# Attention and two gated networks on one core: the normed tokens turned on another path, the values a step later

## The reference, cut to what matters

```python
xn = layernorm(x)
# attention: 8 heads of 128, chunks of 128 tokens, linear attention with a running state
h  = rmsnorm(xn, attn_norm_w)
q, k, v = h @ Wq, h @ Wk, h @ Wv
for each chunk:                      # per head
    o = tril(q @ k.T) @ v + q @ S
    S = S + k.T @ v
o  = rmsnorm(o, attn_out_norm_w)     # per head
x2 = xn + o @ Wo
h2 = rmsnorm(x2, mlp_norm_w)
s  = x2 + (silu(h2 @ Wgate) * (h2 @ Wup)) @ Wdown
# second network: activations and weights rounded to FP4 in groups of 16
g  = silu(fp4_linear(silu(fp4_linear(xn, w_gate)) * fp4_linear(xn, w_up), w_down))
out = x + s * g
```

## Time and profile before

| | |
|---|---|
| median of 3 runs (lowest, highest) | 1065.48 us (1065.27, 1066.4) |
| the profiled execution | 1066.6 us |
| its span, first to last instruction | 1064.5 us |
| attention phase, 64 steps | 22 to 606 us |
| networks phase | 606 to 1064 us |
| TensorE / VectorE / ScalarE busy | 99% / 85% / 50% |
| granted TensorE clock, mean | 0.999 of full |
| DMA | 143 MB, 134 GB/s |

### The profile page before, as it was taken

One profiled execution on the slowest core, in us unless ns is written; L12 is line 12 of the kernel. 1 busy time (PEld: TensorE's weight loads), 2 busy tenths in 40 slices (PEclk: granted clock), 3 DMA queues, 4 the chain that ended last, 5 costly groups with the idle time before them and its releaser, 6 DMA issues.

```text
span 1064.5 us, 18767 instructions
## 1 busy us (share of the span) xinstructions
PE 1053.9 (99%) x6794; PEld 961.5 (90%) x6794; DVE 908.8 (85%) x1887; ACT 528.1 (50%) x1490; POOL 47.4 (4%) x68
## 2 busy tenths in 40 slices
PE   9999999999999999999999999999999999999998
PEld 5999999989999989989999889999999999999997
DVE  6788888888888888888888798888888888889887
ACT  6664655756656546557555634443333333243332
POOL 0000000000000000000000000101001010101010
PEclk9999999999999999999999999999999999999999
DMA  7445355455464553653544623253433233423213
GB/s 237 149 159 174 108 173 168 138 157 166 134 192 133 165 171 115 187 170 123 171 148 162 194 66 99 80 158 93 121 90 119 85 120 97 122 84 92 87 57 112
DMA packets 166173, 143.08 MB, mean 134 GB/s; under 512 B 28737, under 2 KB 162881, under 8 KB 166081
## 3 DMA queue, kind: packets, MB, share of 16 engines
q1 hardware_dynamic: 166080, 141.88, 42.7%
HBM read 77.27 MB, written 64.57 MB: 133 GB/s over the span
## 4 chain that ended last, share of the span: by engine, by line
PE 88%; DMA 6%; DVE 2%; ACT 2%; SPq 2%; issue 1%; DVEq 0%
PE ps L259 69%; PE ps L713 5%; PE ps L757 4%; PE ps L751 4%; PE ps L737 4%; DMA moved<-work 3%; DMA r_gate<-moved 2%; SPq L409 1%; PE ps L839 1%; PE ps L598 1%; SPq L481 1%; DMA work<-kept_w 1%; DMA work<-in_L_attn_hidden_states 0%; ACT work L922 0%; DVE work L1473 0%
## 5 line engine op out<-in xcount | busy, mean ns | idle before, releaser
L259 PE MATMUL ps<-r_k,r_gate_up 128*128 128x512 f32 x768 | 185.2, 391 | 0.5 <-DVE r_k L1537 0.5
L259 PEld LDWEIGHTS ps<-r_k,r_gate_up 128*128 128x128 f32 x768 | 141.5, 188 | 27.9 <-issue 0.7
L259 PE MATMUL ps<-r_o,onT 128*128 128x256 f32 x768 | 107.0, 289 | 0.4 <-DVE onT L1265 0.4
L259 PE MATMUL ps<-r_h,r_k 128*128 128x512 f32 (+1 forms) x393 | 105.2, 403 | 0.0
L259 PEld LDWEIGHTS ps<-r_q,r_v 128*128 128x128 f32 x768 | 99.7, 191 | 5.0 <-DVE r_v L1605 0.3
L259 PE MATMUL ps<-r_q,r_v 128*128 128x256 f32 x768 | 102.3, 283 | 0.0
L259 PE MATMUL ps<-r_h,r_q 128*128 128x512 f32 x384 | 98.2, 391 | 0.0
L946 ACT ACTIVATE work<-ps 128x128 f32<-128x128 f32 x256 | 67.0, 276 | 62.8 <-PE ps L757 62.7
L259 PE MATMUL ps<-r_v,r_h 128*128 128x512 f32 x384 | 97.4, 390 | 0.0
L259 PEld LDWEIGHTS ps<-r_o,onT 128*128 128x128 f32 x768 | 95.8, 190 | 0.8 <-DVE onT L1265 0.7
L922 ACT ACTIVATE work<-ps 128x512 f32<-128x512 f32 x64 | 38.3, 599 | 109.3 <-PE ps L259 109.1
(11 more groups left out here) (155 smaller groups left out, 1996.1 us busy)
## 6 DMA issues: line engine op xcount, KB each, us to landing
moved<-work SPq DMA_DIRECT2D x63, 512.0 KB, 2.9
r_gate<-moved SPq DMA_DIRECT2D x252, 128.0 KB, 2.5
kept_h<-work SPq DMA_DIRECT2D x31, 384.0 KB, 2.6
work<-kept_h SPq DMA_DIRECT2D x124, 96.0 KB, 2.3
work<-in_L_attn_hidden_states SPq DMA_DIRECT2D x16, 512.0 KB, 5.4
kept<-work SPq DMA_DIRECT2D x9, 514.0 KB, 4.4
kept_h<-work SPq DMA_DIRECT2D x9, 512.0 KB, 3.6
kept_xq<-work SPq DMA_DIRECT2D x8, 512.0 KB, 5.8
```

What stands on the lines that cost most here:

```text
L259: done = pe.matmul(out_ap, a, b, start=first and n == 0, stop=last and n == 2, skip_group_check=skip)
```

## The change

It does five things.

1. `turn_h` is gone from TensorE after the first block. VectorE turns `h_sb` in 32x32 blocks into `x_in` at step 3 (early), SP stores it to `kept_h` within that step's `exchange`, then loads it into `xq_new` in four parts behind that exchange; ScalarE and VectorE make the parts of `hT` from there at step 4.
2. The weight of the attention norm no longer scales `hT` but Wq, Wk and Wv, once at the start. `nw_attn` is loaded by a DMA on ScalarE's queue.
3. Values are made one step later than before (`values_of`), since `hT` is ready later. In steps 0 and 4 they stand between keys and queries.
4. VectorE's extras move: `x2_factor` from early to late step 3, the piece's scales from late step 7 to early step 0, its grid to late step 1, the rounding of x and the transposes of h2 about one step later. h2 is now normed in place in `x2`, after `x2` is stored, at step 5.
5. On SP's queue the store of h2 moves from step 5 to 6.

```diff
-                def exchange(value, o=None, turned_o=None, again=True):
+                def exchange(value, o=None, turned_o=None, again=True, next_h=None):
...
+                    if next_h is not None:
+                        sp.wait_ge(h_turned, KD + next_h)
+                        sp.dma_start(kept_h[next_h % HALVES].rearrange("a p x -> p a x"),
+                                     in_quads(x_in.rearrange("p c d -> p (c d)"))).then_inc(h_stored, 16)
                     if again:
                         sp.wait_ge(k_tok_ready, value - 1)
...
+                        if turns_h:
+                            if 1 <= n <= PIECES:
+                                sp.wait_ge(grid_read, n)
+                            if n:
+                                sp.wait_ge(xq_ready, n)
+                            sp.wait_ge(h_stored, 16 * (n + 1))
+                            load_turned(xq_new, kept_h[(n + 1) % HALVES], h_loaded)
...
+        def values_of(b, j):
+
+            h, s = j % H, j // H
+            if 0 < h <= CH:
+                return 1, h - 1, s
+            if h == 0:
+                return (0, CH - 1, s) if b or j else None
+            return (0, h - CH - 1, 1 - s) if b * HALVES + s < BLOCKS - 1 else None
...
-                    if h == CH and ahead:
-                        pe.wait_ge(hT_ready, (n0 + s) * KD + 2 * KD)
...
                         project(wk, B_K, h_next, s_next, k_done)
+                    v = values_of(b, j)
+                    if v is not None and h % CH == 0:
+                        pe.wait_ge(v_ready, t0 + j - 1 + CH)
+                        values(*v)
+                    if not (final and last):
                         project(wq, B_Q, h_next, s_next, q_done)
-                    pe.wait_ge(v_ready, min(CH, STEPS - j) + t0 + j if final else t0 + j + CH)
-                    if ahead or h < CH:
-                        values(*((1, h, s) if h < CH else (0, h - CH, 1 - s)))
+                    if v is not None and h % CH:
+                        if h == CH + 1:
+                            pe.wait_ge(hT_ready, (n0 + s) * KD + 2 * KD)
+                        pe.wait_ge(v_ready, t0 + j - 1 + CH)
+                        values(*v)
+                    if h % CH == 0:
+                        pe.wait_ge(v_ready, t0 + j + CH)
...
-                    if h == CH - 1 and ahead:
-                        pe.wait_ge(h_ready, n0 + s + 2)
-                        pe.wait_ge(k_perm_ready, t0 + j + 2)
-                        turn_h(0)
-                        pe.wait_ge(attn_ready, t0 + j + 1)
-                        turn_h(1)
...
+                def turned_hi(parity, n):
+                    act.wait_ge(h_loaded, 16 * QUADS * n)
+                    for k in range(KD):
+                        act.activation(as_tokens(hT[:, parity, HI, k, :]), landed(xq_new, k), ACT.Copy).then_inc(hT_hi, 1)
...
-                    if h == CH - 1 and ahead:
-                        turned_hi(0, 1 - s, (n0 + s) * KD + KD + 1)
-                        turned_hi(1, 1 - s, (n0 + s) * KD + KD + 2)
...
+                    if h == CH and ahead:
+                        turned_hi(1 - s, n0 + s + 1)
...
+                    if h == CH + 1 and ahead:
+                        normed_h2(n0 + s + 1, None)
...
                     if h == 0 and rounds_piece:
-                        dve.wait_ge(xq_ready, n)
-                        fp4_grid(piece, grid_w, mine)
+                        fp4_scales(piece, piece, scale, mine)
...
-                    if h == 3:
-                        x2_factor(n + 1, mine)
-                    if h == 3 and rounds_piece:
+                    if h == CH - 1 and rounds_piece:
                         fp4_add(piece, grid_w, mine, ALU.subtract)
+                        dve.sem_inc(grid_read, 1)
+                    if h == CH - 1 and ahead:
+                        dve.wait_ge(h_ready, n + 2)
+                        turn_blocks(x_in.rearrange("p c d -> p (c d)"), h_flat, h_turned)
...
                     if h == (0 if final else CH):
                         fp4_max(x_of_block, x_scale, mine)
-                    if h == CH + 1:
-                        if rounds_piece and n <= KD:
-                            weights4_lo(n - 1, h_flat[:, 0:N4])
-                            dve.wait_ge(w4_ready, n)
-                        elif rounds_piece:
+                    if h == (0 if final else CH + 1):
+                        fp4_factor(x_scale, mine)
+                    if h == CH + 2 and not final:
+                        if n > KD and rounds_piece:
                             dve.wait_ge(piece_stored, 16 * (n - KD))
-                        if not final:
-                            turn_h2(n)
-                    if h == CH + 2 and not final:
-                        fp4_add(xq_new, grid_x, mine)
+                        turn_h2(n, x2[:, :, 0:D])
                     if h == CH + 3 and not final:
-                        dve.wait_ge(h2_stored, 16 * n + 16)
-                        turn_xq(n)
+                        fp4_scaled(xq_new, x_scale).then_inc(x_rounded, 1)
...
-                    if h == CH - 1 and ahead:
-                        turned_lo(0, 1 - s, n * KD + KD + 1)
-                        turned_lo(1, 1 - s, n * KD + KD + 2)
+                    if h == CH - 1:
+                        x2_factor(n + 1, mine)
                     if h == CH - 1 and rounds_piece:
                         settled(fp4_scaled(piece, scale), mine)
+                    if h == CH and ahead:
+                        turned_lo(1 - s, n + 1)
```

## The result

The kernel after took 1068.86 us at the median (1065.76 to 1071.31 in 20 runs) beside 1066.09 for the kernel before on the same chip (1064.17 to 1068.97 in 20). The ratio is 1.0024, 95% interval 1.0015 to 1.0033: slower by 2.6 us where I had forecast 3.9 faster, and above the 1066.5 at which my range ended. A second timing gave 1.0011 (0.9999 to 1.0024), so the loss is 1 to 3 us. The profiled execution has a span of 1067.1 beside 1064.5.

The account below looks back on a forecast made before the run. TensorE, busy 99% of the span, was taken as the bound, VectorE second. Terms -6.1 + 2.1 - 1.6 + 1.7 - 0.3 + 0.3 = -3.9 gave a median of 1061.6 us; 8-in-10 range 1059 to 1066.5.

Parts of the forecast that it names:

- The transposes and their cover: Step 3: eight TensorE transposes gone in blocks 0 to 6, -6.1; state sums then late in blocks 1 to 6, +2.1.
- Step 5: Blocks 1 to 3: weight-split and h2 transposes leave the place ahead of the state sums, -1.6.
- The new transfers: Store and loads of turned tokens on SP's queue, steps 3 and 4: land before ScalarE comes at 6.4, cost 0.
- Rival 2: Added transfers slow only exchanges, delaying turn_k of step 5: +2 to +5 in all, no change that can be told; chance 0.26.
- Step 4's order: Step 4 of the odd blocks: VectorE's chain begins 0.1 later, adding 0.2.
- Step 6: 2.6 to 3.5 of rounding behind step 5's sums; step 6's sums still reached under the limits, nothing lost.
- Step 0: Scale instructions ahead of the sums: 0.2 in five blocks, 0.8 in block 5; fp4_factor in the last block, +0.5.
- the values: Values one step later: -1.1 in block 0's step 0, +0.8 in the last block's step 4; -0.3 together.
- The start: Weight scaling by halves +0.2, attention weight's load beside x +0.1 (bounds 0 and 0.5); +0.3 together.

Follow-up runs that it names:

- The last experiment: Step 3's second addition (line 1371) put behind the state sums, on the kernel after with reduction and attention weight's load already moved later; ratio to before 0.9953, 1061.54 us.
- small trip: Kernel after with the turned tokens' store and loads cut to a sixteenth, hT made from unturned tokens; ratio to the kernel before 0.9996.

## Why the prediction was wrong, step by step

**The transposes and their cover: right in sum, partly by luck.** -6.1 + 2.1 = -4.0 was forecast. Block 0's step 3 gave 0.86, the others went from 5.21 to 2.57 and 2.05: -3.5 and -4.0. The sums began at 6.81 or 6.82 in blocks 2 and 4 as forecast (6.80), 6.31 in the odd ones. The last experiment shows that the wait was VectorE's order. Block 5 is the exception (10.19 and 9.58 for 9.1): a packet of q8 started 4.5 and 4.4 into step 2, while that step's exchange store was in flight, and its loads went out at 8.42 and 7.75 instead of 6.62. So the sum of the new waits, 2.6 and 2.1 for the forecast 2.1, is right by two errors that cancel: blocks 1 and 3 lost 0.13 to 0.15 each for the forecast 0.60 and 0.33, and block 5 lost 1.28 and 0.67 for 0.18.

**Step 5: right.** -1.6 was forecast; it went from 1.67 and 1.26 to 0.01.

**The new transfers: this step failed.** I costed them at nothing, for one reader alone: ScalarE in turned_hi. On that I was right; its copy (line 930) began 6.29 into step 4 without a wait:

```profile
355.15 1.14 ACT L930 ACTIVATE r_h<-work 128x512 fp32r<-128x512 f32 x2
```

What I left out is the exchange that the store meets in its own step. Rival 2 had contention, but put it a step too late (step 4's store, turn_k of step 5) and let it reach no change at worst. Step 4 alone lost 3.9, and 3.0 of it went away with the bytes. "The exchange's loads begin at 6.70 anyway" was true and not enough; when they land was the question, and against a step end that comes 0.56 to 0.87 sooner. The rows had it: the last load of the earlier trace rows is issued at 345.97 and lands 2.5 later, at 348.5, and turn_k started at 349.74. That is 1.2 of cover. The shorter step takes 0.6 of it and the later landing 1.8 (12.80 for 10.96 after step 3's start: 0.45 in issuing, 1.4 in flight), so turn_k comes 1.2 later. The instruction packet is part of that 1.4: without one the last load was in flight 3.1 to 3.4. The prediction has nothing on the packets, and the rows of the kernel before don't tell where they fall in the kernel after.

**Step 4's order: about right where it can be read.** I gave it 0.2, for the odd blocks. In the small trip blocks 1 and 5 lost 0.12 and 0.19, against 0.03 and 0.10 before, and blocks 4 and 6 nothing. Its block 2 waited 0.21 for a transfer. Block 3 lost 0.60, 0.36 of it because VectorE began its normalisation at 0.70 instead of 0.34, after 0.59 idle, though ScalarE's root had ended at 0.24; why stays open.

**Step 6: failed, small.** I wrote "nothing". Sums came at 6.48 in block 1 and 7.28 in block 2, 0.3 and 0.8 lost. VectorE of the kernel after, block 2: step 5 ends at 220.59.

```profile
219.03 0.88 DVE L1518 TENSOR_TENSOR r_up<-work,r_up 128x704 fp32r<-128x704 f32 x1
219.94 1.22 DVE L1360 TENSOR_TENSOR work<-work 128x1024 f32<-128x1024 f32 x1
221.20 0.69 DVE L1367 TENSOR_SCALAR work<-work 128x1024 uint32<-128x1024 uint32 x1
221.92 0.69 DVE L1368 TENSOR_SCALAR work<-work 128x1024 f32<-128x1024 f32 x1
...
225.89 1.26 DVE L1444 STREAM_TRANSPOSE work<-work 128x512 f32<-128x512 f32 x2
...
227.87 0.94 DVE L1567 TENSOR_TENSOR work<-ps,work 128x128 f32<-128x128 f32 x3
```

The 3.5 of work behind the sums was counted, but the transposes of h2 that now stand ahead of the next ones (225.89) were not added to it.

**Step 0 and the values.** Block 7's step 0 took 9.12 (forecast 9.4), so that term is 0.2 and not 0.5. Block 5's 0.8 can't be judged: its step 0 was 10.66 and 9.27 in two executions of the kernel before. The 0.8 at step 60 came. The 1.1 at the start came too, as 1.24, and went again: step 1 took 9.11 for 7.49. Step 1 needs the exchange that step 0 starts, and that one hangs on the start. In the kernel after turn_k waits 1.70 for it, and the second exchange's loads took 2.47 to issue:

```profile
29.46 2.47 SPq L424 DMA_DIRECT2D r_gate<-moved  x4
```
```profile
34.83 0.71 DVE L1400 STREAM_TRANSPOSE work<-r_gate 128x512 f32<-128x512 f32 x1 [1.70 <-DMA r_gate<-moved]
```

**The start: mis-sized.** 0.1 for the weight's load beside x; it is 0.5, the end of the bounds that I had given.

**The sum** of the parts that repeat is -3.8 (step 3), -1.5 (step 5), +3.8 (step 4), +0.8 (step 6), +0.8 (step 60), +0.7 (start): +0.8, on the mean of two executions of each kernel. Steps 0 and 1 and the last steps add what differs between executions, here some 3.6 us (4.4 in all at the end of step 62). The timings say +1.2 and +2.6. How much of the steps 0 and 1 is the change's own remains open.

## What to carry to other kernels

Before taking work off the full engine, list what else used its time as cover, not only the second engine but each transfer in flight, and hold its landing against the new end of the step. When a transfer is added, look first at the one beside it in the same step, and at what stands between that landing and the full engine; here one reduction of 1.18 that depended on neither decided between a gain of 3 us and a loss of 2. Steps in the same place of the loop repeat between executions to a few tenths here, while single late transfers move by 1 or 2 us, so a second profile of the same program is worth its run before a difference is explained. And look at where the packets of the instruction queue fall: they keep their places within a few tenths in versions of one program, and move when the instructions of the loop change, so two kernels can differ by them; no run here moved one alone.

## What the runs showed of the hardware

A load of 1 KB in 256 pieces on ScalarE's queue beside a 512 KB load on SP's delayed the large one by 0.5 to 0.9 us (5.58 to 5.71 in eight profiles, 4.81 to 5.04 in five without it); with the small one issued 1.4 later it was 5.03 in one version and 5.38 in another. The Trainium skill ("DMA: Bandwidth & Descriptors", Queues, rings and completion order) says that each DMA engine goes round between the queues it has work for, packet by packet; the trace agrees in kind.

SP needs 0.43 us to issue one of these loads; four took 1.73 to 1.76 in most steps, but 2.1 to 2.45 where a 512 KB store had been issued some 0.5 ahead of them in the same queue (2.43 above; 1.76 with the store issued 1.4 ahead, in the last version). The 3.04 above had a packet of the instruction queue besides, at 346.7, 0.4 ahead of the first load. At about 29 us, with no store beside them, four took 2.0 to 3.0 in every kernel that has a packet of the instruction queue between 28 and 32 us (the line below, kernel after), and 1.73 in both executions of the kernel before, in the one with the transfers added and in the last version, which have none there. That the fetch of instructions causes it is argued from where the packets fall; no run moved one on purpose.

```profile
q8 instruction: 1, 0.02, 2.7%
```

The Trainium skill ("Runtime: NRT & Kernel Launch", Instruction fetch mechanics) calls the cost of crossing into a new block of instructions "mostly hidden". Here the four issues took 0.2 to 1.2 longer in those windows, and step 1 of block 0 was behind them.

The same packets go with late landings. In the fifteen profiles, between 40 and 590 us, the exchange's 512 KB store landed after 3.6 to 5.1 us (median 4.4, 86 cases) when a packet of q8 had started 0.3 to 2.0 after its issue, and after 2.92 at the median (631 cases) when none was near. For the last of the four loads the medians are 3.6 (209 cases) and 2.7 (557).
